# Weighted and attribute passes of a graph network: a group's eight sums between the second and the third fetched chunk of the next group

## The reference, cut to what matters

```python
# L0, two layers: one weight for each edge
msg = h[src] * edge_weight[:, None]
h_neigh = segment_sum(msg, dst, n) * inv_deg
h = h @ W_self[l].T + h_neigh @ W_neigh[l].T + b_neigh[l]

# L1, two layers: 64 coefficients for each edge, from an attribute array
a = a_mu + exp(a_ls) * edge_attr
m = (h * norm_out)[src] * a
agg = segment_sum(m, dst, n)
h = agg * norm_in @ W + b
```

## Time and profile before

| | |
|---|---|
| median of 3 runs | 11507.88 us |
| the profiled execution's own time | 11493.85 us |
| its span | 11492.0 us |
| PE, matmuls | 7803.2 us, 68% of the span |
| DVE | 7897.7 us, 69% |
| POOL | 5213.4 us, 45% |
| ACT | 2331.1 us, 20% |
| mean granted TensorE clock, as a share of 2.4 GHz | 0.788 |

### The profile page before, as it was taken

The page is one execution under the profiler, slowest core; times in us unless marked ns, Lnnn a source line. Parts: engine busy times, 40 slices in busy tenths (PEclk is TensorE's granted clock), DMA queues, the critical chain, the costliest instruction groups (busy, mean ns, idle before and its releaser), DMA issues. The chain is left out here.

```text
span 11492.0 us, 176718 instructions
## 1 busy us (share of the span) xinstructions
PE 7803.2 (68%) x44549; PEld 5533.5 (48%) x44550; DVE 7897.7 (69%) x11191; ACT 2331.1 (20%) x8740; POOL 5213.4 (45%) x5215
## 2 busy tenths in 40 slices
PE   6888899788878875565477556546745555655557
PEld 4666677566656663333266223226722233522226
DVE  7777555577667776777899677689855556655558
ACT  1222444200000001111187111117800000000000
POOL 3444555344444435777400577740035552155550
PEclk9999999899999997777655667765566777877678
DMA  2333444344444435777588577757923333333333
GB/s 83 91 92 86 113 121 124 94 117 117 113 101 115 117 93 193 243 247 249 150 331 352 189 247 243 244 154 312 374 72 74 75 76 73 110 74 75 75 70 104
DMA packets 812828, 1718.89 MB, mean 150 GB/s; under 512 B 365243, under 2 KB 447176, under 8 KB 757202
## 3 DMA queue, kind: packets, MB, share of 16 engines
q1 hardware_dynamic: 440902, 1154.81, 28.7%
q0 software_dynamic: 193584, 397.91, 16.4%
q10 hardware_dynamic: 178256, 165.14, 4.3%
HBM read 1273.09 MB, written 444.21 MB: 149 GB/s over the span
## 5 line engine op out<-in xcount | busy, mean ns | idle before, releaser
L693 PE MATMUL ps_G<-table_parts,low_onehots 125*128 125x320 bf16 x21840 | 3373.4, 314 | 531.4 <-issue 248.4
L528 POOL DMA_INDIRECT gathered_rows<-node_table,index x2080 | 1981.0, 952 | 2205.0 <-PE ps_sum L548 1477.3
L693 PEld LDWEIGHTS ps_G<-table_parts,low_onehots 125*128 125x128 bf16 x21840 | 2181.8, 102 | 1571.9 <-issue 319.5
L528 POOL DMA_INDIRECT gathered_rows<-xl_table,index x1664 | 1836.2, 1103 | 1579.4 <-PEq L1498 931.8
L528 POOL DMA_INDIRECT gathered_rows<-rel_table,index x1456 | 1386.5, 952 | 2142.0 <-ACT index L518 1165.8
L1510 PE MATMUL ps_Z<-xr,onehots_wide 125*128 x3328 | 1443.6, 590 | 1070.8 <-issue 603.9
L548 PE MATMUL ps_sum<-messages,onehots 128*125 128x65 f32 (+3 forms) x13312 | 1949.6, 310 | 242.7 <-DVE messages L1907 181.8
L548 PEld LDWEIGHTS ps_sum<-messages,onehots 128*125 128x125 f32 x13312 | 1877.9, 226 | 317.8 <-issue 302.9
L723 DVE TENSOR_TENSOR rows_by_feature<-ps_G,fifth_onehots 128x320 f32<-128x320 f32 x1456 | 706.7, 485 | 1638.6 <-remote 950.0
L1510 PEld LDWEIGHTS ps_Z<-xr,onehots_wide 125*128 125x128 f32 x3328 | 775.9, 247 | 1738.5 <-issue 1616.0
L1558 DVE TENSOR_TENSOR z<-gathered_rows,ps_Z 128x650 f32<-128x650 f32 x832 | 661.5, 825 | 694.1 <-issue 409.9
(11 more groups left out here) (328 smaller groups left out, 7044.8 us busy)
## 6 DMA issues: line engine op xcount, KB each, us to landing
stash_a<-gathered_rows SPq DMA_DIRECT2D x208, 1300.0 KB
kept_rows<-stash_a SPq DMA_DIRECT2D x208, 1300.0 KB
onehots<-onehots_kept SPq DMA_DIRECT2D x520, 500.0 KB
onehots_turned<-onehots_turned SPq DMA_DIRECT2D x416, 250.0 KB
low_rows<-low_rows SPq DMA_DIRECT2D x416, 187.5 KB
stash_r<-gathered_rows ACTq DMA_DIRECT2D x208, 272.0 KB
kept_rows<-stash_r SPq DMA_DIRECT2D x208, 272.0 KB
onehots_kept<-onehots ACTq DMA_DIRECT2D x104, 500.0 KB
```

The costliest lines, as they stand in the source:

```text
L528: pool.indirect_dma_start(G[:, HALF * k + q, 0:width], None, table, bass.IndirectOffsetOnAxis(IDX[:, k, q:q + 1], 0)).then_inc(gathered[k] ...
L693: last = nc.tensor.matmul(ps_G[:, (fetch * k + g) % 2, 0:D * FIVE], OT[0:BN, k, g, a, :], HP[:, part, a, :, :].rearrange("p f b -> p (f b) ...
```

## The change: the third fetch moves behind the sums

`fetch_rows` gets a parameter that says which of the three chunks of a group it fetches. In `weighted_sums` and in `attribute_sums` TensorE now has, in group k: the first and second fetch of group k+1, the sums of k, the third fetch of k+1. The number of instructions is the same. What waits for what is the same too: a fetch still waits for its bank, the sums for the messages, the picks for the fetch.

```diff
-        def fetch_rows(pe, OT, HP, ps_G, i, k, fetch=FETCH):
+        def fetch_rows(pe, OT, HP, ps_G, i, k, fetch=FETCH, some=None):
 
             i, k = i + k // K, k % K
             n = K * i + k
-            pe.wait_ge(low_made.sem, low_made.at(n + 1))
-            for g in range(fetch):
+            some = range(fetch) if some is None else some
+            if 0 in some:
+                pe.wait_ge(low_made.sem, low_made.at(n + 1))
+            for g in some:
                 pe.wait_ge(bank_picked.sem, bank_picked.at(fetch * n + g - 1))
...
                                 if not (last_turn and k == K - 1):
-                                    fetch_rows(pe, OT, HP, ps_G, i, k + 1)
+                                    fetch_rows(pe, OT, HP, ps_G, i, k + 1, some=range(FETCH - 1))
                                 if hist:
...
                                 last.then_inc(chunk_done.sem, HALF)
+                                if not (last_turn and k == K - 1):
+                                    fetch_rows(pe, OT, HP, ps_G, i, k + 1, some=range(FETCH - 1, FETCH))
```

## The result

The changed kernel took 11532.92 us (median of 20 runs) beside 11490.74 for the kernel before (20 runs): a ratio of 1.0038, with a 95% interval of 1.0028 to 1.0049. The profiled execution after has a span of 11529.8 us against 11492.0, 37.8 more.

The account below looks back on a forecast made before the run. The prediction took TensorE's waits for VectorE's picks, delayed by GpSimd's gathers, to bound the kernel. First weighted pass +196, attribute passes -244, second weighted pass -37 gave -85 us: 11409 profiled, 11423 as median, range 11340 to 11505.

Parts of the forecast that it names:

- The first weighted pass's chain: First weighted pass: third fetch, pick, one-hots, ScalarE's messages and sums in one chain, 10.78 us a group against 9.50 before.
- The price of the clock in it: First weighted pass: TensorE's 2.42 us idle drops its clock every second group at 1.2 us, 0.60 a group.
- The attribute passes: Both attribute passes: period falls from 9.75 and 9.60 to 8.50 us a group, together 244 us saved.
- The hold: TensorE signals falling into the later part of GpSimd's five gathers are seen only about 7.30 us after these began.
- The two equations: Attribute passes: period 7.84 plus the third fetch's wait, and held picks timing that fetch, together give 8.40 us.
- the wait ahead of the third fetch: Attribute passes: w, the time TensorE's third fetch waits after the sums; p = 7.84 + w, with p 8.40.
- groups that slip: Attribute passes: allowance of 0.10 us a group added to the period of 8.40, giving 8.50.
- The second weighted pass: Second weighted pass: period falls from 9.21 to 8.85 us a group, 37 us saved (0 to 60).
- the caught signal: Attribute passes: slower rival, third fetch's signal held, about 5 us per caught group; 11633 at a fifth of them; chance 0.13.
- No fall of the clock: First weighted pass: rival that the clock stays up, so 62 us go and the time is 11361; chance 0.20.
- The hold catches the third fetch: Attribute passes: slower rival, third pick 5.5 us late in caught groups; gain gone from 17 of 208 groups; chance 0.13.
- There is no hold: Attribute passes: rival that only VectorE's lateness counts, 8.26 us a group, 50 us more saved, 11373; chance 0.05.

Follow-up runs that it names:

- e3: Changed kernel plus twelve unused TensorE matmuls in each group of the first weighted pass, ahead of the wait for messages: 10593.0 us, ratio 1.0249.
- e9: Changed kernel with one gather in place of five per group in the attribute passes (result not the networks'): 11337.9 us, ratio 0.9958.
- e10: Kernel before with one gather in place of five per group in the attribute passes (result not the networks'): 11042.67 us, ratio 0.9698.
- e16: Changed kernel, ScalarE making messages before its one-hot waits and stores in both weighted passes; repeat run beside a kernel before at 11375.41: 11014.15 us, ratio 0.9687.
- e17: Changed kernel with the old order back in the first weighted pass only, third run, beside a kernel before at 11375.41: 11121.69 us, ratio 0.9779.
- e5: The changed kernel itself, unaltered, again, beside a kernel before at 10330.16: 10746.03 us, ratio 1.041.
- e1: Changed kernel with the old order back in the first weighted pass only, beside a kernel before at 10340.32: 10376.97 us, ratio 1.004.
- e2: Kernel before with the new order in the first weighted pass alone: 10730.29 us, ratio 1.0379.
- e6: Kernel before (old order everywhere), ScalarE making messages before the one-hot wait and store in the first weighted pass: 10320.29 us, ratio 0.9998.
- e4: Changed kernel, ScalarE making messages before the one-hot wait and store in the first weighted pass: 10370.56 us beside 10340.32, ratio 1.0034.
- e15: Changed kernel, ScalarE making messages before its one-hot waits and stores in both weighted passes: 10348.94 us beside 10334.67, ratio 0.9998.

## Why the prediction was wrong

**The first weighted pass's chain: right.** Forecast 10.78 us a group and 2.42 idle ahead of the sums; measured 10.7 where the clock holds, 10.80 in e3, and 2.26 idle, ended by ScalarE's messages.

**The price of the clock in it: the step that failed.** "I take a fall in every second group at 1.2 us ... 0.60 a group". The term measured 1.40 (12.20 against e3's 10.80), and the pass's clock 0.87, not 0.93. How often the clock falls was about right: 57 of 100 groups are slow. The price of one fall was not: the slow groups take 13.3 us on average, 2.5 more than e3's 10.80, where 1.2 was taken and 1.63 was the upper end. The reason given for 1.2 was that some of the slow stretch lies on the first fetch, which is not in the chain. But the fetch that follows the sums is now the third, which is in the chain; at 503.30 it took the slow stretch from its start, and its pick came 1.67 later than in the earlier trace rows. And at 514.26 the sums themselves, which are in the chain too, ran 1.66 longer. The price came from one slow fetch in an attribute pass, and the slow stretch can cover more than one fetch. By the windows the pass cost 280 us in place of 196. The term's upper end, 1.63 in every group, lies near the 1.40 by luck: it has too many falls at too low a price.

**The attribute passes: mechanism right, size off.** The hold is real (e9, e10), and the third fetch's signal escapes it. The period was 8.68 beside the result, 207 us saved in place of 244, and 8.52 and 8.51 in e16 and e17, where 8.50 was forecast. The two equations let only signals wait, and the sums break as well. In the windows of the first attribute pass TensorE's idle time inside the sums, with no releaser, is 44.5 us in 96 groups beside the result, 24.9 in 83 in e16, 22.1 in 70 in e17, and there is none in e5; its waits for VectorE's picks are 12.7, 15.4, 14.9 and 23.1. So the longer breaks account for the 0.16 between 8.68 and 8.52; why they are longer is open. The forecast had 0.55 a group for the wait ahead of the third fetch, which measured 0.13, and added 0.10 for groups that slip without a row for it, so that it came near 8.52 is partly luck.

**The second weighted pass: right beside the result.** 8.85 forecast and measured, 37 us. The period in the new order is 8.75 to 8.85 in every set with the hold; the gain depends on the old order, which took 9.21 here and 8.74 in e10. Why is open.

The sum on the profiled execution: -85, plus 84 for the first pass, plus 37 for the attribute passes, is +36; the spans say +37.8. The clock's price alone takes the forecast gain to about nothing; with the shorter gain of the attribute passes it is a loss. The range was too narrow for its own terms. Its stated upper ends, 1.2 a group for the clock and 8.7 for the attribute period, add up to 11423 + 62 + 42 = 11527, and all adverse ends of the parts together give +163, but the range stopped at 11505, below the time of the kernel before: it went up for the caught signal, not for the clock's own end.

**The rivals.** "No fall of the clock" is false; e3, which forces it, gives 10.80. "The hold catches the third fetch" is false: the pick at 2703.36 comes 2.32 after its fetch, and the waits of all 96 groups average 0.94. "There is no hold" is false beside the result, but in the sets without it the attribute groups take 8.22, where that rival said 8.26. The Trainium skill (SBUF — State Buffer, SBUF: two separate sides) says of the engines' ports to SBUF that TensorE never waits for anyone there. In e5 the trace agrees, with no idle time inside the sums of the first attribute pass; beside the result TensorE stands idle inside them for 44.5 us, and no run shows whether a port is what it waits for. What I had not thought of is that the whole gain hangs on an effect that some sets of runs do not have. Without it the old order takes 8.50, 8.27, 8.22 and 8.21 us a group (e1's first pass, the others from e2 and e6), and the change can only lose.

## What to carry to other kernels

Before an order is changed so that a long chain closes behind the last wait, work out the idle time that it leaves on TensorE in one piece, and ask which instructions come right behind it. If they are in the chain, the whole slow stretch is: here 2.5 us for a slow group, where a single slow fetch had shown 1.63. Look for what stands in the chain without belonging to it: here ScalarE's wait and store ahead of the messages, whose move took the pass from 12.2 to 8.5 us, without the hold (e4) and with it (e16). And a gain that rests on one stall should be measured where the stall is absent too.

## What the runs showed of the hardware

- Five gathers in a row can hold TensorE's signals until 7.0 to 7.5 us after the first of them began, and break a run of matmuls on TensorE until 7.0 to 7.3 us after it. With one gather in a row this did not show (e9, e10).
- The hold is not a fixed trait: the kernel before took 10330 to 10340 us in some sets and 11375 to 11491 in others, and both the set of e9 and e10 (with it) and that of e15 (without) ran on a chip numbered 15. What switches it is not known, and nothing here tried it.
- A repeated idle time of 2.26 us a group on average brought the clock of a pass to 0.87, one of 1.44 to 0.95, and one of 0.63 left it at 1.00. The clock fell after some idle times of 2.20 us and not after others. Useless matmuls in the gap made the pass 11% shorter (e3).
